# Attention scores taken in pairs of PSUM banks: one maximum and one exponential for two units, one mask for four

## What is computed

```python
attn = softmax(einsum('bnd,bmd->bnm', q, k) * scale)          # first pass
out = einsum('bnm,bmd->bnd', attn, v) @ proj_w.T + proj_b
sim_tokens = out / maximum(norm(out), EPS)                    # per head
sim = einsum('bnd,bmd->bnm', sim_tokens, sim_tokens) * 10.0
sim = softmax(where(sim < 0, -inf, sim))                      # second pass
out2 = einsum('bnm,bmd->bnd', sim, v) @ proj_w.T + proj_b
```

## Time and profile before

| | |
|---|---|
| median of 3 runs | 654.46 us (653.89 to 654.61) |
| the profiled execution | 653.99 us, of which the span of the trace is 652.2 us |
| PE busy in the span | 546.4 us (84%) |
| DVE busy | 435.3 us (67%) |
| ACT busy | 340.5 us (52%) |
| POOL busy | 228.6 us (35%) |
| share of the chain that ended last | PE 62%, DVE 22%, issue 5%, DMA 5%, ACT 3% |

### The profile page before, as it was taken

The page is one execution under the profiler, slowest core; times in us unless marked ns, Lnnn a source line. Parts: engine busy times, 40 slices in busy tenths (PEclk is TensorE's granted clock), DMA queues, the critical chain, the costliest instruction groups (busy, mean ns, idle before and its releaser), DMA issues.

```text
span 652.2 us, 11861 instructions
## 1 busy us (share of the span) xinstructions
PE 546.4 (84%) x3482; PEld 326.3 (50%) x3483; DVE 435.3 (67%) x870; ACT 340.5 (52%) x794; POOL 228.6 (35%) x278
## 2 busy tenths in 40 slices
PE   0657799988999899999979887605999999999991
PEld 0323323432344324433343332503899999999990
DVE  3488987888798999997688975289333343434330
ACT  1221676677788888779968764100343433333340
POOL 6850421417051240104113300003165655556541
PEclk9965999999999999999999987555999999999997
DMA  4191043135444090402342577902123323232321
GB/s 114 47 118 23 30 71 49 30 70 92 55 60 88 18 126 6 107 1 52 47 106 49 80 240 168 309 1 77 28 45 56 48 50 55 43 56 42 52 33 16
DMA packets 40562, 45.00 MB, mean 69 GB/s; under 512 B 10404, under 2 KB 34854, under 8 KB 40519
## 3 DMA queue, kind: packets, MB, share of 16 engines
q0 software_dynamic: 12864, 19.97, 18.2%
q1 hardware_dynamic: 27654, 24.52, 17.4%
HBM read 17.88 MB, written 7.60 MB: 39 GB/s over the span
## 4 chain that ended last, share of the span: by engine, by line
PE 62%; DVE 22%; issue 5%; DMA 5%; ACT 3%; POOL 0%; POOLq 0%; DVEq 0%; ACTq 0%; SPq 0%
PE psum L1108 11%; PE psum L960 10%; PE psum L1092 7%; DVE MX L736 5%; PE psum L1021 5%; PE psum L997 5%; PE psum L1097 4%; PE psum L1028 4%; PE psum L1013 4%; DVE arena L750 4%; PE psum L1050 3%; DMA result<-T,slot_dest 3%; PE psum L985 3%; PE psum L1039 1%; PE psum L1060 1%
## 5 line engine op out<-in xcount | busy, mean ns | idle before, releaser
L584 ACT ACTIVATE arena<-psum 128x512 f32<-128x512 f32 x384 | 206.8, 613 | 42.8 <-PE psum L1021 27.3
L736 DVE TENSOR_REDUCE MX<-psum 128x1 f32<-128x512 f32 x192 | 123.4, 680 | 8.1 <-PE psum L1013 7.9
L750 DVE SCALAR_TENSOR_TENSOR arena<-arena 128x1024 f32<-128x1024 f32 x96 | 120.4, 1266 | 11.3 <-ACT arena L584 10.8
L616 ACT ACTIVATE arena<-psum,b_sb 128x128 f32<-128x128 f32 x234 | 64.8, 377 | 108.1 <-PE psum L1097 108.0
L960 PE MATMUL psum<-arena 128*17 128x512 f32 x768 | 102.6, 606 | 5.4 <-DVE arena L750 5.4
L499 POOL DMA_INDIRECT result<-T,slot_dest x39 | 64.8, 1662 | 77.6 <-DVE T L927 55.3
L1108 PE MATMUL psum<-arena 128*128 x468 | 86.4, 335 | 0.6 <-ACT arena L616 0.6
L360 POOL DMA_DIRECT2D KS<-arena x72 | 36.9, 514 | 118.0 <-PE psum L1028 58.9
L1108 PEld LDWEIGHTS psum<-arena 128*128 128x128 f32 x468 | 75.0, 190 | 5.5 <-issue 1.1
L483 POOL DMA_INDIRECT xg_sb<-x_rows,slot_token x39 | 39.6, 1015 | 87.2 <-DVE slot_dest L882 75.7
L1013 PE MATMUL psum<-late_stacks,arena 96*128 96x512 bf16 x144 | 58.2, 414 | 12.8 <-DMA late_stacks<-arena 7.2
(11 more groups left out here) (172 smaller groups left out, 659.1 us busy)
## 6 DMA issues: line engine op xcount, KB each, us to landing
late_stacks<-arena POOLq DMA_DIRECT2D x72, 64.0 KB, 4.3
QS<-arena SPq DMA_DIRECT2D x72, 64.0 KB, 3.6
KS<-arena POOLq DMA_DIRECT2D x72, 64.0 KB, 3.6
arena<-w SPq DMA_DIRECT2D x8, 576.0 KB, 8.1
arena<-arena SPq DMA_DIRECT2D x54, 64.0 KB, 4.4
arena<-w SPq DMA_DIRECT2D x8, 384.0 KB, 6.2
x_rows<-X SPq DMA_DIRECT2D x4, 384.0 KB, 2.8
result<-H SPq DMA_DIRECT2D x4, 384.0 KB, 3.1
```

The costliest lines, as they stand in the source:

```text
L584: act.activation((P1, P2)[ps][:, n % PRING, :], s, ACT.Exp, scale=(QSCALE, SIM_SCALE)[ps]).then_inc(done, 1)
L616: last = act.activation(HT[i][:, hc, :], hid_ps[i][hc], ACT.Gelu, bias=b1_sb[:, bass.ds(e, 1), hc:hc + 1].rearrange("p o h -> p (o h)"))
L736: dve.tensor_reduce(MX[:, g % 2, CT * i + c:CT * i + c + 1], slot(k), AX_X, ALU.max).then_inc(freed[k % RING], 1)
L750: dve.scalar_tensor_tensor(p, p, 1.0, p, ALU.is_ge, ALU.mult).then_inc(masked, 1)
```

## The change

Two units of a kind are handled as one pair in two neighbouring banks: two matmuls, then one `tensor_reduce` over both banks, or one `activation` over both. A mask handles four units (128 x 2048). S of a `q` moves to a quarter step after the step (it had its two halves at 0 and 1/2), and E of a `q` stays at its first half's time. The bank of each PSUM unit comes from a table: a pair starts at an even bank, so where the next free bank is odd, it is left out; a single unit takes one bank. Before it fills its banks, PE waits for the last user of each.

```diff
-            for j in range(2):
-                at(a + q + j / 2, 2, "max_unit", g, q, j)
-                at(a + OFF_C + q + j / 2 - 0.25, 3, "exp_unit", g, q, j)
-                at(a + OFF_E + q + j / 2, 4, "sim_unit", g, q, j)
-            at(a + OFF_E + q + 1.25, 0, "mask", g, q)
+            at(a + q, 2, "max_pair", g, q)
+            at(a + OFF_C + q - 0.25, 3, "exp_pair", g, q)
+            at(a + OFF_E + q + 0.25, 4, "sim_pair", g, q)
+            if q % 2:
+                at(a + OFF_E + q + 1.25, 0, "mask", g, q)
...
+def place_units():
+
+    bank, turn, before = [], [], []
+    turns, last, free = [0] * RING, [None] * RING, 0
+    for kind, args in UNIT:
+        width = 2 if kind in PAIRS else 1
+        if free % width:
+            free = (free + 1) % RING
+        banks = range(free, free + width)
+        before.append(sorted({last[x] for x in banks if last[x] is not None}))
+        for x in banks:
+            last[x] = len(bank)
+        bank.append(free)
+        turn.append(turns[free])
+        turns[free] += 1
+        free = (free + width) % RING
+    return bank, turn, before
...
-                        if n >= PRING:
-                            act.wait_ge(pv_done[ps], (n - PRING) // GH + 1)
-                        act.activation((P1, P2)[ps][:, n % PRING, :], s, ACT.Exp,
+                        if n >= PRING:
+                            act.wait_ge(pv_done[ps], (n - PRING) // GH + 1)
+                        act.activation((P1, P2)[ps][:, n % PRING:n % PRING + 2, :], slot_pair(k), ACT.Exp,
                                        scale=(QSCALE, SIM_SCALE)[ps]).then_inc(done, 1)
...
-                        dve.tensor_reduce(MX[:, g % 2, CT * i + c:CT * i + c + 1], slot(k), AX_X, ALU.max
-                                          ).then_inc(freed[k % RING], 1)
+                        dve.tensor_reduce(MX[:, g % 2, CT * i + c:CT * (i + 1) + c + 1:CT], slot_pair(k), AX_X, ALU.max
+                                          ).then_inc(freed[BANK[k]], 1)
...
-                        wait_consumed(dve, unit("sim_unit", g, q, 0))
-                        wait_consumed(dve, unit("sim_unit", g, q, 1))
-                        n = 2 * (UG * g + q) % PRING
-                        p = P2[:, n:n + 2, :]
+                        wait_consumed(dve, unit("sim_pair", g, q - 1))
+                        wait_consumed(dve, unit("sim_pair", g, q))
+                        n = 2 * (UG * g + q - 1) % PRING
+                        p = P2[:, n:n + 4, :]
                         dve.scalar_tensor_tensor(p, p, 1.0, p, ALU.is_ge, ALU.mult).then_inc(masked, 1)
...
-                            pe.wait_ge(masked, UG * g + 2 * (c + 1))
+                            pe.wait_ge(masked, CT * g + c + 1)
...
-                    if k >= RING:
-                        wait_consumed(pe, k - RING)
+                    for n in BEFORE[k]:
+                        wait_consumed(pe, n)
...
-                        last = pe.matmul(s, QS[0][sl][0:SD, i, c * P:(c + 1) * P], KS[0][sl][0:SD, i, :], start=True, stop=True)
+                        for j in range(2):
+                            i = (2 * q + j) % GH
+                            last = pe.matmul(slot_pair(k)[:, j, :], QS[0][sl][0:SD, i, c * P:(c + 1) * P], KS[0][sl][0:SD, i, :], start=True, stop=True)
```

More of the change, by code:

```diff
@@ L135 @@
 EVENTS = schedule()
-PSUM_KINDS = ("x_transpose", "q_proj", "k_proj", "v_proj", "max_unit", "max_row", "exp_unit", "normalise",
-              "o_transpose", "proj_norm", "t_transpose", "sim_unit", "proj_out", "gate_transpose", "gate_logits")
+PSUM_KINDS = ("x_transpose", "q_proj", "k_proj", "v_proj", "max_pair", "max_row", "exp_pair", "normalise",
+              "o_transpose", "proj_norm", "t_transpose", "sim_pair", "proj_out", "gate_transpose", "gate_logits")
 UNIT = {ev: k for k, ev in enumerate(e for e in EVENTS if e[0] in PSUM_KINDS)}
+PAIRS = ("max_pair", "exp_pair", "sim_pair")
+def place_units():
[14 more added lines that the diff above has]
+    return bank, turn, before
+BANK, TURN, BEFORE = place_units()
 SPLIT = {ev: k for k, ev in enumerate(e for e in EVENTS if e[0] in ("q_proj", "k_proj", "t_transpose"))}
@@ L286, in slot, with slot_pair @@
         def slot(k):
[L287 removed]
+            return psum[:, BANK[k], :]
+        def slot_pair(k):
+            return psum[:, BANK[k]:BANK[k] + 2, :]
         def slot_tiles(k):
[L291 removed]
+            return psum[:, BANK[k], 0:2 * C].rearrange("p (c d) -> p c d", c=2)
         hid_ps = [[psum[:, 2 * i + hc // HB, hc % HB * P:(hc % HB + 1) * P] for hc in range(HC)] for i in range(2)]
@@ L332, in wait_filled @@
         def wait_filled(e, k):
-            e.wait_ge(filled[k % RING], k // RING + 1)
+            e.wait_ge(filled[BANK[k]], TURN[k] + 1)
         def wait_consumed(e, k):
-            e.wait_ge(freed[k % RING], k // RING + 1)
+            e.wait_ge(freed[BANK[k]], TURN[k] + 1)
         def part_rows(nm, g):
@@ L356, in load_part @@
             eng.wait_ge({"H": hi_written, "M": mid_written, "L": lo_written}[parts[r]], n + 1)
-            last_reader = ("exp_unit", "sim_unit")[ps]
+            last_reader = ("exp_pair", "sim_pair")[ps]
             if g >= SLOTS[ps]:
-                wait_filled(eng, unit(last_reader, g - SLOTS[ps], UG - 1, 1))
+                wait_filled(eng, unit(last_reader, g - SLOTS[ps], UG - 1))
             eng.dma_start(dst[g % SLOTS[ps]][r * D:(r + 1) * D, :, :].rearrange("d h n -> d (h n)"),
@@ L546, in _ @@
                     k = unit(kind, *args)
-                    done = freed[k % RING]
+                    done = freed[BANK[k]]
                     s = slot(k)
@@ L950, in _ @@
                             for q in (2 * c, 2 * c + 1):
-                                for j in range(2):
-                                    wait_consumed(pe, unit("exp_unit", g, q, j))
+                                wait_consumed(pe, unit("exp_pair", g, q))
                             wait_consumed(pe, unit("v_proj", b, c // 2))
                         else:
-                            pe.wait_ge(masked, UG * g + 2 * (c + 1))
+                            pe.wait_ge(masked, CT * g + c + 1)
                         if c == 0 and g >= 1:
@@ L1018, in _ @@
                             pe.wait_ge(stack_ones_set, SLOTS[0])
-                        if (q, j) == (0, 0):
+                        if q == 0:
                             pe.wait_ge(row_loaded[sl], 32 * (g // SLOTS[0] + 1))
-                        last = pe.matmul(s, KS[0][sl][:, i, c * P:(c + 1) * P], QS[0][sl][:, i, :], start=True, stop=True)
-                    elif kind == "sim_unit":
-                        g, q, j = args
-                        i, c, sl = (2 * q + j) % GH, q // 2, g % SLOTS[1]
-                        if (q, j) == (0, 0):
+                        for j in range(2):
+                            i = (2 * q + j) % GH
+                            last = pe.matmul(slot_pair(k)[:, j, :], KS[0][sl][:, i, c * P:(c + 1) * P], QS[0][sl][:, i, :], start=True, stop=True)
+                    elif kind == "sim_pair":
+                        g, q = args
+                        c, sl = q // 2, g % SLOTS[1]
+                        if q == 0:
@@ L1026, in _ @@
                             for side in "qk":
                                 pe.wait_ge(sim_loaded[side][sl], LOADS * (g // SLOTS[1] + 1))
-                        last = pe.matmul(s, QS[1][sl][:, i, c * P:(c + 1) * P], KS[1][sl][:, i, :], start=True, stop=True)
+                        for j in range(2):
+                            i = (2 * q + j) % GH
+                            last = pe.matmul(slot_pair(k)[:, j, :], QS[1][sl][:, i, c * P:(c + 1) * P], KS[1][sl][:, i, :], start=True, stop=True)
@@ L1031, in _ @@
                         for q in range(UG - 2, UG):
-                            for j in range(2):
-                                wait_consumed(pe, unit("max_unit", g, q, j))
+                            wait_consumed(pe, unit("max_pair", g, q))
                         last = pe.transpose(s[0:4 * GH, 0:P], MX[:, g % 2, :], ident[:, :])
@@ L1061, in _ @@
                                                  start=kc == 0, stop=kc == KC - 1)
-                    last.then_inc(filled[k % RING], 1)
+                    last.then_inc(filled[BANK[k]], 1)
                 chose = rt["b"][:, :, :].rearrange("p t e -> p (t e)")
```

44 lines of the change are left out of this document (21 added, 23 removed).

## The result

The changed kernel takes **700.03 us** (median of four runs, 698.67 to 702.22); the kernel before took 654.17 in the same comparison. The ratio is 1.0713, with a 95% interval of 1.0673 to 1.0753. The forecast was 678 us with 698 for its upper end: the direction was right, the loss of 46 us is nearly twice the 24 of the sum, and the time lies just outside the range. The profiled execution took 700.27 us, its span is 698.5.

A forecast was written before the change was run, and what follows sets the result against it. PE and DVE, both near full, were taken to bound the kernel. Terms of 8 + 5 + 8 + 3 = 24 us on the profiled 653.99 us gave 678 us; likeliest case 662 to 698, whole range 647 to 698.

The forecast's parts named there:

- M with E: Stretch with M and E: M waits for an earlier E, two steps 3.26 us instead of 2.83; 5 us lost.
- What bounds the kernel: PE and DVE both near full with all three kinds; PE sets M and E's pace, masks set S's.
- What the change saves: Longer DVE instructions save at most 0.08 us each, 144 times: 11.5 us if all on the path.
- All three kinds: Stretch with M, E and S: two steps take 5.21 us instead of 4.68; 8 us lost.
- the refill of M: With all three kinds, an emptied pair is ready after 0.70 us, so every second maximum waits; 0.53 us per two steps.
- its cover is PE's 2.39 us a step: Paired exponentials on ACT, busy 110 of 135 us with all three kinds, bound nothing; costed at nothing.
- S alone: S running alone: the mask needs all four exponentials, two steps 3.0 us instead of 2.27; 8 us lost.
- E with S: Stretch of 30 us with E and S: PE needs 1.95 us a step, ACT 1.86; unchanged.
- Singles: A transpose, projection or `max_row` in the ring costs a whole pair's place; 3 us lost, between 0 and 8.
- The faster case: Rival: DVE's other work mostly covers the refills, so saved instruction time counts; 642.5 or 646 us, chance 0.19.
- The falling clock: Rival: PE's new gaps bring the half clock to all of S alone; 10 us more, 688 us, chance 0.06.

The follow-up runs named there:

- e2: Kernel before with the changed order of M, S and E alone, single units and masks of two kept: 659.65 us, ratio 1.011.
- e5: Changed kernel with M in single units and masks of two units again, only E and S as pairs: 674.35 us, ratio 1.035.
- e1: Changed kernel with masks of two units again, pairs for maxima and exponentials kept: 680.16 us, ratio 1.047.
- e4: Changed kernel with M in single units again, E, S and masks as changed: 692.68 us, ratio 1.067.
- e6: Changed kernel with the first matmul of E done five times at five places to keep PE busy: 697.9 us, ratio 1.072.
- e3: Changed kernel with a pair allowed to start at any bank but the last: 701.89 us, ratio 1.079.
- e12: Kernel before with its two masks of two units side by side where the mask of four stands: 673.39 us, ratio 1.033.
- e11: Kernel before with masks of four units, placed half a step later in the order: 673.67 us, ratio 1.035.

## Why the prediction was wrong

Put in a row, the runs split the change into four parts, in us of the stages (of one execution each) and as a step of the ratio:

| part | from, to | M+E | 3 kinds | rest | ratio |
|---|---|---|---|---|---|
| order | before, e2 | 6.1 | 0.3 | 2.5 | +0.011 |
| pairs of E and S | e2, e5 | 3.0 | 8.0 | 2.4 | +0.024 |
| pairs of M | e5, e1 | 6.3 | 0.6 | -1.3 | +0.012 |
| masks of four | e1, after | 0.0 | 7.8 | 10.9 | +0.024 |
| sum | | 15.4 | 16.7 | 14.5 | +0.071 |
| forecast | | 5 | 8 | 8 | +0.036 (3 more for singles) |

The clock is inside these parts. The time at the half clock, in M with E, with three kinds and in the rest, is 0, 0 and 9.7 us before; 3.4, 0 and 3.4 in e2; 0, 0 and 6.8 in e5; 6.8, 0 and 3.4 in e1; 6.8, 6.8 and 8.9 after. If PE set the pace throughout, half of such a time would be lost: an estimate, and the most that it can be. So up to 1.7 of the 6.1 for the order, 3.4 of the 6.3 for pairs of M, and 3.4 of the 7.8 and 2.7 of the 10.9 for masks of four are the clock, which fell behind the new waits.

- **What bounds the kernel**, and the durations: right. Maxima 1.23 (1.21), masks 2.28 (2.26), exponential pairs 1.02 on the page (1.05; the prediction's own rows give 0.61 + 0.52 = 1.13, so this one was nearer than its working).
- **What the change saves**: sized right, about 10 us of DVE time (11.5), and worth nothing, as it turned into idle time. The Trainium skill (Perfetto Trace Analysis, Optimizing Scalar/DVE Operations) gives overheads by which 15 us would have been saved, an estimate from that page; DVE's busy time fell by 10.0. Its other sentence there, that smaller instructions let work finish sooner where other engines wait, is what these runs show, e1 by some 16 us.
- **All three kinds** (8; measured 16.7). The loop is right: 5.25 against 5.21, gap 0.70. But the refill of M, on which the whole term rested, is worth at most 3.2 us there with masks of four (e4, the clock included) and 0.6 with masks of two (e1 against e5). What was missing are two parts costed at nothing: the exponentials ("its cover is PE's 2.39 us a step"), 8.0 us, and the mask, whose length I had priced only as a saving of 0.08, 7.8 us. Neither shows in a plain loop. Both show in the steps with other work, where singles, norms and splits want a bank or DVE at the wrong time.
- **M with E** (5; measured 15.4). The loop is right, 3.25 against 3.26. The failed step is "so many have other work between ... I take half": the steps with other work lost too, and more each than a plain one; all 21 double steps in full would be 9. 6.1 us come from the order alone, which had no term, and some 3 of the 6.3 for pairs of M from the clock (e6).
- **S alone** (8; measured 10.5). The mechanism is right, and the size nearly. The loop takes 3.0 us; the six short intervals (2.0 to 2.5 us before) pay 0.77 each, where 0.73 was forecast. The others pay 0.45 each and not "part, 0.3". 8.0 of the 10.5 us go with the masks of four (e1).
- **E with S** (nothing; measured 4.3 with what follows up to S alone). Its plain loop is indeed "unchanged", 1.96 us between two `pv` before and 1.95 after. The intervals around it aren't: the dearest grows by 1.36 us.
- **Singles** (3): a place left out costs nothing that e3 could show. What singles pay is the whole pair's exponential, counted above.
- **The rivals.** The faster case rested on DVE's other work covering the refills; it doesn't. The falling clock was placed in S alone, where both kernels have two such spells; it fell in M with E and with three kinds instead, for about 3 us in the first and 1 to 3 in the second.

So the failed step is one and the same in both stretches where M runs: the plain loop's loss was taken for the largest, and other work between steps for a cover. It was the reverse. A plain double step of M with E pays 0.41 us between its `pv`; the one from 116.39 us on, full of other work, pays 2.29 (6.82 before, 9.12 after). In the plain loops everything is periodic and the wait has its place; the mixed steps had lived on the freedom of six single banks and of short DVE instructions. Only in S alone did the plain loop pay the most.

## What to carry to other kernels

Merging instructions of an engine that isn't the only bound coarsens two things at once, how soon a buffer comes back and how long the engine's queue is held; price both at the small instructions and odd users of the buffers between the loops, and not in the loop alone. A saving per instruction (10.0 us of DVE's time over 144 instructions here, 0.07 each) is worth looking for only where the engine has no idle time ahead of its waits. If such a merge is tried, test it by bunching the old instructions at the new one's place: e12 showed what the mask of four costs with three kinds without the mask of four. And look at PE's rows behind each new wait: a part of what a wait costs can be the clock that falls after it.

## What the runs showed of the hardware

- **The clock can fall behind a short idle time of PE, and does not always.** In the changed kernel stretches of some 3 us at the half clock, with rows about twice as long (the `pv` 1.91 for 1.05 us), stand behind idle times of 1.27 to 2.8 us, and one (163.63) behind three shorter ones (0.59, 0.75 and 0.45 us). Record and rows agree on the place: the mean granted clock is 1.00 from 126.0 to 129.5, 0.50 from 129.6 to 133.0 and 1.00 again from 133.1 on. But the clock stays full behind the 1.75 us ahead of 151.18 and the 2.41 ahead of 366.86, and what decides is open.
- **DVE and POOL in each other's way.** In e12 the two masks of two that start at 225.63 take 4.17 us, where 2.3 is usual, and in e11 a mask of four and POOL meet. POOL and DVE in e11:

```profile
227.16 1.15 POOL L352 TENSOR_TENSOR arena<-arena 128x512 bf16<-128x512 f32 x1 [0.28 <-ACT arena L537]
...
228.99 3.05 POOL L352 TENSOR_TENSOR arena<-arena 128x512 bf16<-128x512 f32 x1 [0.22 <-ACT arena L537]
```

```profile
228.76 2.27 DVE L753 SCALAR_TENSOR_TENSOR arena<-arena 128x2048 f32<-128x2048 f32 x1
```

POOL's addition starts 0.23 us behind the mask and takes 3.05 instead of 1.15 us: it ends at 232.04, 1.01 behind the mask's end (231.03), as if it had begun only then. The Trainium skill (SBUF — State Buffer, Who interferes with whom) says that a DVE instruction with two inputs in SBUF contends with a GpSimd one that reads SBUF, and that such contention is an exclusive lock; the rows agree. So a longer mask also holds POOL longer, which I had not priced, and no run here sizes that by itself.
